# Reciprocal roots of a layer norm on VectorE alone, and one inverse-transform bank moved, in a Fourier-layer tokenizer

## The chip, the cores and the metric

The kernel runs on one core of a Trainium2 chip. The metric is the device time of one execution in microseconds (us); the runs of a kernel are summed up by their median.

## The reference, cut to what matters

The model turns 64 images of 64 x 64 x 3 into 64 x 64 tokens with a small Fourier network (32 channels, 4 layers), then runs an attention block, a gated feed-forward block, a linear recurrence and a mixture of experts over the tokens. The change lies in the tokenizer:

```python
def layer_norm(x, g, b):
    mu = jnp.mean(x, axis=-1, keepdims=True)
    var = jnp.mean((x - mu) ** 2, axis=-1, keepdims=True)
    return (x - mu) * jax.lax.rsqrt(var + EPS) * g + b
...
h = layer_norm(x @ fc0_w + fc0_b, ln0_g, ln0_b)
h = jnp.transpose(h, (0, 3, 1, 2))
for i in range(LAYERS):
    w1 = w1r[i] + 1j * w1i[i]
    w2 = w2r[i] + 1j * w2i[i]
    x1 = spectral_conv(h, w1, w2)
    x2 = jnp.einsum('bchw,oc->bohw', h, conv_w[i]) + conv_b[i][None, :, None, None]
    h = x1 + x2
    h = jnp.transpose(h, (0, 2, 3, 1))
    h = layer_norm(h, ln_g[i], ln_b[i])
    if i < LAYERS - 1:
...
```

`spectral_conv` is a two-dimensional Fourier transform of which 24 x 12 modes are kept, a 32 x 32 complex mixing of channels for each mode, and the inverse transform. Every layer norm needs one reciprocal root for each pixel.

## The kernel before, in words

**Tiling.** The 64 images go in 4 groups of 16, and a group in 2 units of 8 images. A group runs an embedding stage, three layers in a hardware loop, a last layer and the MLP (`program`, line 821); each stage does unit 0 and then unit 1. For each of them there is a *main pass* (`pe_main`, `act_main`, `dve_main`, `pool_main`): one for each unit in the embedding, in each of the three layers and in the last layer, 10 in a group, 40 in all. In the embedding and the three layers a *forward transform* follows (`pe_forward`, `drain_forward`), 32 in all: row transform (line 508), column transform (line 522), mixing (line 539).

**A main pass** handles 16 chunks of 128 partitions x 512 columns. The engines run instruction lists written out by hand and meet at semaphores only:

- TensorE writes chunk c into one of six PSUM banks (`wide[c % 6]`: four of `main`, two of `aux`). In the embedding that is one matmul (line 446), in the layers an inverse column transform (line 453) and a channel matmul (line 456). A bank is written again only when the chunk six before it has been scaled (`main_free`).
- ScalarE squares the bank into `sq` (line 725), VectorE sums the squares over 32 channels (line 703). The means are already zero, since the weights are centred.
- The roots come in two ways. For chunks 0 and 1 of every four, GpSimd adds EPS (line 757) and raises to the power -0.5 (line 760), one chunk at a time. For chunks 2 and 3, VectorE runs nine small instructions for both chunks together behind the reduce and the scaling of the fourth (`dve_newton`, lines 662 to 679).
- VectorE scales chunk c - 3 behind the reduce of chunk c (`scale`, line 694, with `wait_rstd`), into one of two `xn` buffers. After the last reduce the scalings 13, 14 and 15 follow.
- TensorE transposes the scaled chunk (line 464), five chunks later in its own list; ScalarE applies gain, bias and GELU (line 737). In the three layers TensorE also transposes the result back (line 472) and ScalarE copies it into `pix` (line 743); the row transform reads that.

**Inverse row transform.** Towards the end of a main pass TensorE also does eight banks of the *next* unit's inverse row transform (`pe_inverse`, line 423) in the two `aux` banks, even ones drained by VectorE, odd ones by ScalarE (`drain_inverse`, line 598). `inv_banks(c)` says which bank belongs behind which step of the list: banks 0 to 3 behind steps 15 to 18, banks 4 and 5 behind step 19, 6 and 7 behind step 20. In the layers step 21 has only the last transposes back. Bank 0 waits until chunk 11 has been scaled, since `aux` held chunks 10 and 11.

The forward transform begins with a wait for both drains:

```python
            if nxt is not None:
                for j in range(2):
                    pe.wait_ge(inv_free[j], inv_of(g, *nxt) + AX_C)
```

In the embedding it then transposes 64 tiles (line 495) in turn through two `aux` and two `tp` banks; in the layers it starts at the row transform, whose results go to `main[0]` and `main[1]`. The column transform uses `main[2]`, `main[3]`, then `tp`, and for its last third (y = 2) the two `aux` banks.

The spectrum goes out and back by DMA on SP's queue (`sp_spectrum`), for use by the inverse banks of the next main pass. A line of the profile that belongs to a helper (598 is `copy`) holds many tiles.

Of the kernel before, what the change touches and what calls it, by code (L numbers as in the profile page):

```python
# [106 lines left out]
def tokenizer(nc, t, tok, named):  # L107
# [9 lines left out]
    with ctx:  # L117
# [31 lines left out]
        mhalf = sb("mhalf", [128, 16])  # L149
# [56 lines left out]
        with nc.Block() as block:  # L206
# [43 lines left out]
            def _(dve):  # L250
# [6 lines left out]
                dve.memset(mhalf[:, :], -0.5)  # L257
# [76 lines left out]
        main_full, main_free, sq_full, red_done, var_done, rstd_done, newton, tp_full, tp_free = (  # L334
            sem(n) for n in ("main_full", "main_free", "sq_full", "red_done", "var_done", "rstd_done", "newton",
# [43 lines left out]
        def inv_banks(c):  # L379
            return {NCH - 1: (0,), NCH: (1,), NCH + 1: (2,), NCH + 2: (3,), NCH + 3: (4, 5), NCH + 4: (6, 7)}.get(c, ())  # L380
# [49 lines left out]
        def pe_main(pe, g, s, u, l, nxt):  # L430
# [7 lines left out]
            for c in range(NCH + LAG + (1 if turns else 0)):  # L438
# [36 lines left out]
                if nxt is not None:  # L475
                    for k in inv_banks(c):
# [137 lines left out]
        def drain_forward(eng, j, g, s, u, l):  # L614
            _, n = base_of(g, s, u, l)
            fwd = (g * (LAYERS * UNITS) + (0 if s == 0 else l * UNITS + UNITS) + u)
            if s == 0:
                n = n + AX_EMBED
                for k in range(j, 4 * AX_ROWS, 2):
# [3 lines left out]
                    else:  # L623
                        eng.wait_ge(row_full[j], (g * UNITS + u) * AX_ROWS + (START + k // 4 + 1))
                    copy(eng, j, pv[:, :, :, 4 * k:4 * k + 4].rearrange("p c a r -> p a c r"),
                         (aux if first else tp)[j][:, :].rearrange("p (r a c) -> p a c r", r=4, a=NA)).then_inc(
# [27 lines left out]
        def dve_newton(dve, m, c):  # L654
# [8 lines left out]
            dve.wait_ge(main_free, after(m, c, 4))  # L663
            dve.wait_ge(newton, done + 4)
            dve.tensor_scalar(y.bitcast(I32), v.bitcast(I32), -0.5, float(0x5f3759df), ALU.mult, ALU.add).then_inc(newton, 4)
            dve.wait_ge(newton, done + 8)
            dve.tensor_tensor(w, y, y, ALU.mult).then_inc(newton, 4)
            dve.wait_ge(newton, done + 12)
            dve.tensor_tensor(w, w, v, ALU.mult).then_inc(newton, 4)
            dve.wait_ge(newton, done + 16)  # L670
            dve.scalar_tensor_tensor(out=w, in0=w, scalar=-10 / 3, in1=w, op0=ALU.add, op1=ALU.mult).then_inc(newton, 4)
            dve.wait_ge(newton, done + 20)
            dve.scalar_tensor_tensor(out=y, in0=w, scalar=5.0, in1=y, op0=ALU.add, op1=ALU.mult).then_inc(newton, 4)
            dve.wait_ge(newton, done + 24)
            dve.scalar_tensor_tensor(out=w, in0=y, scalar=-0.5 * CUBIC ** 2, in1=y, op0=ALU.mult, op1=ALU.mult).then_inc(newton, 4)
            dve.wait_ge(newton, done + 28)
            dve.tensor_tensor(w, w, v, ALU.mult).then_inc(newton, 4)
            dve.wait_ge(newton, done + 32)
            dve.scalar_tensor_tensor(out=y, in0=w, scalar=1.5, in1=y, op0=ALU.add, op1=ALU.mult).then_inc(newton, 4)

        def wait_rstd(dve, m, c):

            if c % 4 < 2:
                dve.wait_ge(rstd_done, m + 4 * (c // 4) + 2 * (c % 4 + 1))
            else:
                dve.wait_ge(newton, (m - START) * NEWTON_OPS + (START + (c // 4 + 1) * 4 * NEWTON_OPS))

        def dve_main(dve, g, s, u, l, nxt):
# [10 lines left out]
            for c in range(NCH):  # L699
# [7 lines left out]
                if c % 4 == 3:  # L707
# [8 lines left out]
        def act_main(act, g, s, u, l, nxt):  # L716
# [4 lines left out]
            for c in range(NCH + LAG + (1 if turns else 0)):  # L721
                if c < NCH:
# [3 lines left out]
                                   scale=CH ** -0.5 / (CUBIC if c % 4 >= 2 else 1)).then_inc(sq_full, 1)  # L726
# [18 lines left out]
                if nxt is not None:  # L745
                    for k in inv_banks(c - 1):
                        if k % 2:
                            drain_inverse(act, 1, g, *nxt, k)
            if nxt is not None and not turns:
                drain_inverse(act, 1, g, *nxt, 7)  # L750

        def pool_main(pool, g, s, u, l):
            m, _ = base_of(g, s, u, l)
            for c in range(NCH):
                if c % 4 < 2:
                    pool.wait_ge(red_done, m + c + 1)
                    pool.tensor_tensor(var[:, c % 4, :], ssum[:, c % 4, :], eps[:, :], ALU.add).then_inc(var_done, 2)  # L757
                    pool.wait_ge(var_done, m + 4 * (c // 4) + 2 * (c % 4 + 1))
                    pool.wait_ge(main_free, after(m, c, 4))
                    pool.tensor_tensor(rstd[:, c % 4, :], var[:, c % 4, :], mhalf[:, :], ALU.pow).then_inc(rstd_done, 2)  # L760
# [927 lines left out]
```

## Time and profile before

| | us |
|---|---|
| median of 3 runs (lowest, highest) | 4886.96 (4884.19, 4889.06) |
| the profiled execution | 4915.42 |
| its span, first to last instruction | 4913.6 |
| TensorE busy | 4008.5 |
| VectorE busy | 2260.9 |
| ScalarE busy | 2096.9 |
| GpSimd busy | 1057.9 |
| mean granted clock of TensorE, as a share of full speed | 0.909 |

The profiled execution took somewhat longer than the runs that were timed without a profile. In a row of the timeline the first number is the start in us from the begin of the span, the second the duration; then engine, line, operation, output <- input, shape, count, and in brackets the idle time of that engine just before it with what ended it. PE is TensorE, DVE VectorE, ACT ScalarE, POOL GpSimd. An fp32 matmul shows as two instructions. In a row of stretches the columns are the stretch, its length, busy us and number of instructions for PE, PE's weight loads, DVE, ACT and POOL, then the granted clock (1.00 is 2.4 GHz, 0.50 is 1.2 GHz), DMA share and GB/s.

### The profile page before, as it was taken

The numbers are of one execution on the slowest core, as the hardware profiler recorded it, in microseconds if no ns is written. First come the engines' busy times: TensorE is split into PE (matmuls) and PEld (weight loads), VectorE is DVE, ScalarE is ACT, GpSimd is POOL, SyncE is SP. The second block draws the span as 40 slices with busy tenths as digits, with TensorE's granted clock in tenths as the row PEclk, the third lists the DMA queues.
The fourth block names the chain that finished last, engine by engine and source line by source line (L and its number), as shares of the span: only waits on it lengthen the run. The fifth ranks groups of instructions, "written<-read, shape, count | busy, mean of one in ns | idle before, by whom it ended". The sixth has DMA issues, their size and how long they took to land. (4 is left out here: it accounts for less than half of the span.)

```text
span 4913.6 us, 101922 instructions
## 1 busy us (share of the span) xinstructions
PE 4008.5 (82%) x39344; PEld 3080.9 (63%) x39344; DVE 2260.9 (46%) x4667; ACT 2096.9 (43%) x3178; POOL 1057.9 (22%) x700
## 2 busy tenths in 40 slices
PE   0189999996899999968999999689999995857268
PEld 0068788842788888427888884278887832853146
DVE  6554443431544345224443442244434422787666
ACT  1254444465544444654443446544444463221113
POOL 0032322321223223212332232223223320000020
PEclk9999999998999999989999999899999997779679
DMA  9501201200022022000210220002102101000000
GB/s 206 159 22 59 79 21 60 79 1 16 21 72 67 21 69 69 1 16 21 79 60 21 75 64 2 15 21 79 60 21 79 59 2 31 1 1 1 0 1 9
DMA packets 168682, 213.28 MB, mean 43 GB/s; under 512 B 156402, under 2 KB 158679, under 8 KB 159874
## 3 DMA queue, kind: packets, MB, share of 16 engines
q1 hardware_dynamic: 166514, 182.84, 12.8%
q10 hardware_dynamic: 1680, 23.60, 1.9%
q8 instruction: 347, 5.69, 0.5%
q14 instruction: 141, 1.16, 0.1%
HBM read 147.28 MB, written 59.12 MB: 42 GB/s over the span
## 5 line engine op out<-in xcount | busy, mean ns | idle before, releaser
L760 POOL TENSOR_TENSOR rstd<-var,mhalf 128x16 f32<-128x16 f32 x320 | 931.2, 2910 | 44.1 <-POOL var L757 4.4
L757 POOL TENSOR_TENSOR var<-ssum,eps 128x16 f32<-128x16 f32 x320 | 69.4, 217 | 2923.9 <-DVE ssum L703 2923.9
L737 ACT ACTIVATE h<-tp,gb 128x512 f32<-128x512 f32 x640 | 553.7, 868 | 297.6 <-PE tp L464 296.1
L703 DVE TENSOR_REDUCE ssum<-sq 128x16 f32<-128x512 f32 x640 | 436.2, 683 | 484.5 <-ACT sq L725 481.0
L508 PE MATMUL main<-fwd_w,pix 128*128 128x96 f32 x4096 | 513.9, 293 | 42.1 <-ACT zq L598 35.1
L508 PEld LDWEIGHTS main<-fwd_w,pix 128*128 128x128 f32 x4096 | 509.6, 209 | 48.8 <-ACT pix L743 40.1
L456 PEld LDWEIGHTS main<-convw,h 128*128 128x128 f32 x3072 | 407.4, 209 | 161.2 <-issue 161.2
L464 PE MATMUL tp<-ident,xn 128*128 128x128 f32 x2560 | 423.6, 292 | 77.5 <-DVE xn L694 71.9
L725 ACT ACTIVATE sq<-main 128x512 f32<-128x512 f32 x480 | 286.5, 599 | 441.2 <-PE main L456 394.3
L456 PE MATMUL main<-convw,h 128*128 (+1 forms) x3072 | 455.7, 300 | 0.0
L423 PE MATMUL aux<-inv_r,yd 96*48 96x64 f32 x8192 | 417.1, 256 | 9.5 <-DVE zq L598 4.5
L464 PEld LDWEIGHTS tp<-ident,xn 128*128 128x128 f32 x2560 | 314.9, 150 | 163.3 <-DVE xn L694 130.6
L423 PEld LDWEIGHTS aux<-inv_r,yd 96*48 96x48 f32 x8192 | 388.9, 185 | 44.7 <-issue 32.5
L453 PE MATMUL main<-zq,inv_w 48*128 48x512 f32 x768 | 292.3, 679 | 88.1 <-DVE xn L694 47.8
L598 DVE COPY t_w<-main 128x384 f32<-128x384 f32 (+1 forms) x192 | 94.2, 490 | 558.3 <-PE main L508 477.4
L694 DVE TENSOR_TENSOR xn<-main,rstd 128x512 f32<-128x512 f32 x480 | 327.0, 683 | 20.3 <-POOL rstd L760 10.9
L598 ACT COPY t_w<-main 128x384 f32<-128x384 f32 (+1 forms) x192 | 81.6, 425 | 580.1 <-PE main L508 479.7
L743 ACT COPY pix<-tp 128x512 f32<-128x512 f32 x384 | 221.4, 576 | 56.0 <-PE tp L472 56.0
L472 PE MATMUL tp<-ident,h 128*128 128x128 f32 x1536 | 241.9, 282 | 0.0
L598 DVE COPY zq<-aux 112x512 f32<-112x512 f32 x128 | 88.1, 688 | 265.6 <-PE aux L423 265.6
L573 PE MATMUL main<-h,f1w 32*128 32x512 f32 x1024 | 181.5, 671 | 14.1 <-ACT pix L768 9.6
L539 PE MATMUL main<-xs,mixw 128*64 128x32 f32 x6144 | 188.9, 223 | 0.0
(240 smaller groups left out, 5868.6 us busy)
## 6 DMA issues: line engine op xcount, KB each, us to landing
mixw<-mix_scratch SPq DMA_DIRECT2D x16, 4608.0 KB, 17.8
y_scratch<-t_w SPq DMA_DIRECT2D x256, 144.0 KB
yd<-y_scratch SPq DMA_DIRECT2D x32, 1152.0 KB, 7.5
mix_scratch<-mixw SPq DMA_DIRECT2D x64, 288.0 KB, 4.8
mixw<-mix_scratch ACTq DMA_DIRECT2D x1, 4608.0 KB, 13.7
h<-in_L_tok_w1r ACTq DMA_DIRECT2D x6, 576.0 KB, 10.1
h<-in_L_tok_w1i ACTq DMA_DIRECT2D x6, 576.0 KB, 10.4
h<-in_L_tok_w2r ACTq DMA_DIRECT2D x6, 576.0 KB, 18.3
```

The source lines that it names most:

```text
L423: mm = pe.matmul(aux[j][64 * half:64 * half + 48, 64 * i:64 * i + 64], ydv[:, u, 8 * e + i, :, :, a].rearrange("p s n -> p (s n)"), inv_r[ ...
L453: pe.matmul(wide[(c + half) % 6][:, :], inv_w[rows, :], zq[rows, 256 * c:256 * c + 512], start=True, stop=False)
L456: mm = pe.matmul(bank[:, 128 * i:128 * i + 128], h[:, (u * S + 4 * c + i) * 128:(u * S + 4 * c + i) * 128 + 128], convw[:, layer, :] if l ...
L464: mm = pe.transpose(tp[0 if turns else d % 2][:, 128 * i:128 * i + 128], xn[:, d % 2, 128 * i:128 * i + 128], ident[:, :])
L472: mm = pe.transpose(tp[1][:, 128 * i:128 * i + 128], h[:, (u * S + 4 * d + i) * 128:(u * S + 4 * d + i) * 128 + 128], ident[:, :])
L508: mm = pe.matmul(main[j][:, 48 * i:48 * i + 96], pv[:, c0 + i, 2 * ap:2 * ap + 2, :].rearrange("p a r -> p (a r)"), fwd_w[:, :], start=Tru ...
L598: return eng.tensor_copy(out, in_) if j == 0 else eng.copy(out, in_)
L694: dve.tensor_tensor(xn[:, d % 2, :].rearrange("p (n c) -> p n c", c=CH), wide[d % 6][:, :].rearrange("p (n c) -> p n c", c=CH), rstd[:, d ...
L703: dve.tensor_reduce(ssum[:, c % 4, :], sq[:, c % 2, :].rearrange("p (n c) -> p n c", c=CH), AX.X, ALU.add).then_inc(red_done, 1)
L725: act.activation(sq[:, c % 2, :], wide[c % 6][:, :], ACT.Square, scale=CH ** -0.5 / (CUBIC if c % 4 >= 2 else 1)).then_inc(sq_full, 1)
L737: act.activation(out, in_, fn, bias=gb[:, 1, stage:stage + 1] if l is None else gb[:, 1, bass.ds(stage, 1)], scale=gb[:, 0, stage:stage + ...
L760: pool.tensor_tensor(rstd[:, c % 4, :], var[:, c % 4, :], mhalf[:, :], ALU.pow).then_inc(rstd_done, 2)
```

## The change

All roots are computed by the nine Newton instructions on VectorE, behind every odd chunk for that chunk and the one before; the instructions have the same shape, 128 x 32, as before. `pool_main`, the GpSimd program that called it, its two semaphores and the constant `mhalf` go. ScalarE's squares get the same scale for all chunks.

In the layers, bank 7 of the inverse row transform moves from step 20 to step 21, behind the last transposes back. The forward transform no longer waits for the drains of the inverse banks at its begin; it waits for them at the first use of `aux` in its column transform (y = 2). For this the embedding's first transposes use `main[0]` and `main[1]` in place of `aux`.

```diff
         def inv_banks(c):
-            return {..., NCH + 3: (4, 5), NCH + 4: (6, 7)}.get(c, ())
+        def inv_banks(c, turns):
+            return {..., NCH + 3: (4, 5), NCH + 4: (6,) if turns else (6, 7), NCH + 5: (7,)}.get(c, ())
...
         def pe_forward(pe, g, s, u, l, nxt):
             m, n = base_of(g, s, u, l)
-            if nxt is not None:
-                for j in range(2):
-                    pe.wait_ge(inv_free[j], inv_of(g, *nxt) + AX_C)
...
-                        mm = pe.transpose((aux if first else tp)[j][:, 128 * i:128 * i + 128],
+                        mm = pe.transpose((main if first else tp)[j][:, 128 * i:128 * i + 128],
...
+                        if nxt is not None and y == 2 and ap == 0:
+                            pe.wait_ge(inv_free[b], inv_of(g, *nxt) + AX_C)
...
         def dve_newton(dve, m, c):
-            v, y, w = (x[:, 2:4, :].rearrange("p k n -> p (k n)") for x in (var, rstd, newton_w))
-            done = (m - START) * NEWTON_OPS + (START + (c // 4) * 4 * NEWTON_OPS)
+            p = slice(c % 4 - 1, c % 4 + 1)
+            v, y, w = (x[:, p, :].rearrange("p k n -> p (k n)") for x in (var, rstd, newton_w))
+            done = (m - START) * NEWTON_OPS + (START + (c // 2) * 2 * NEWTON_OPS)
             dve.wait_ge(red_done, m + c + 1)
-            dve.tensor_scalar(v, ssum[:, 2:4, :].rearrange("p k n -> p (k n)"), EPS / CUBIC ** 2, None, ALU.add).then_inc(newton, 4)
+            dve.tensor_scalar(v, ssum[:, p, :].rearrange("p k n -> p (k n)"), EPS / CUBIC ** 2, None, ALU.add).then_inc(newton, 2)
...
-            if c % 4 < 2:
-                dve.wait_ge(rstd_done, m + 4 * (c // 4) + 2 * (c % 4 + 1))
-            else:
-                dve.wait_ge(newton, (m - START) * NEWTON_OPS + (START + (c // 4 + 1) * 4 * NEWTON_OPS))
+            dve.wait_ge(newton, (m - START) * NEWTON_OPS + (START + (c // 2 + 1) * 2 * NEWTON_OPS))
...
-                if c % 4 == 3:
+                if c % 2:
                     dve_newton(dve, m, c)
...
-                                   scale=CH ** -0.5 / (CUBIC if c % 4 >= 2 else 1)).then_inc(sq_full, 1)
+                                   scale=CH ** -0.5 / CUBIC).then_inc(sq_full, 1)
...
-        def pool_main(pool, g, s, u, l):
...
-                    pool.tensor_tensor(rstd[:, c % 4, :], var[:, c % 4, :], mhalf[:, :], ALU.pow).then_inc(rstd_done, 2)
...
-            @block.gpsimd
-            def _(pool):
...
```

## Rows read from the trace of the kernel before

**Rows 1.** The page, part 1: busy us, share, instructions.
```profile
PE 4008.5 (82%) x39344; PEld 3080.9 (63%) x39344; DVE 2260.9 (46%) x4667; ACT 2096.9 (43%) x3178; POOL 1057.9 (22%) x700
```

**Rows 2.** VectorE's timeline, embedding pass, second unit: start, us, what, idle before.
```profile
318.31 0.69 DVE L703 TENSOR_REDUCE ssum<-sq 128x16 f32<-128x512 f32 x1 [0.17 <-ACT sq L725]
...
322.18 0.17 DVE L662 TENSOR_SCALAR var<-ssum 128x32 f32<-128x32 f32 x1
...
324.69 0.69 DVE L703 TENSOR_REDUCE ssum<-sq 128x16 f32<-128x512 f32 x1
...
325.29 0.68 DVE L694 TENSOR_TENSOR xn<-main,rstd 128x512 f32<-128x512 f32 x1
...
347.46 0.69 DVE L694 TENSOR_TENSOR xn<-main,rstd 128x512 f32<-128x512 f32 x1
```

**Rows 3.** TensorE's timeline, a layer pass.
```profile
501.71 1.12 PE L453 MATMUL main<-zq,inv_w 48*128 48x512 f32 x2 [1.42 <-DVE xn L694]
...
506.50 1.13 PE L453 MATMUL main<-zq,inv_w 48*128 48x512 f32 x4
...
525.89 1.66 PE L423 MATMUL aux<-inv_r,yd 96*48 96x64 f32 x32
```

**Rows 4.** Timelines of TensorE and ScalarE, end of that layer pass.
```profile
543.61 0.66 PE L472 MATMUL tp<-ident,h 128*128 128x128 f32 x4
...
544.30 0.59 ACT L743 COPY pix<-tp 128x512 f32<-128x512 f32 x1 [2.33 <-PE tp L472]
...
545.72 17.55 PE L508 MATMUL main<-fwd_w,pix 128*128 128x96 f32 x128 [1.45 <-ACT zq L598]
```

**Rows 5.** Line 508: TensorE idle before it (us, times), until.
```profile
  ACT zq L598: 35.1, 24
```

**Rows 6.** TensorE's timeline, embedding, second unit: first transposes and row transform.
```profile
361.55 1.06 PE L495 MATMUL aux<-ident,h 128*128 128x128 f32 x8 [0.73 <-issue]
...
369.60 14.50 PE L508 MATMUL main<-fwd_w,pix 128*128 128x96 f32 x128 [0.87 <-ACT pix L598]
```

**Rows 7.** Stretches around 545: us, busy by engine, granted clock, DMA share, GB/s.
```profile
540.00:543.00 3.00, 3.00 (x60) 2.82 (x59) 0.69 (x1) 1.74 (x3) 0.00 (x0) 1.00 0.02 5
...
546.00:548.00 2.00, 2.00 (x11) 2.00 (x11) 0.00 (x0) 0.00 (x0) 0.00 (x0) 0.50 0.00 0
...
552.00:554.00 2.00, 2.00 (x19) 2.00 (x19) 0.00 (x0) 0.48 (x1) 0.00 (x0) 0.97 0.00 0
```

**Rows 8.** Line 508 alone, sums over stretches: 24 in layers, 8 in embeddings.
```profile
sum 480.00, PE 397.88 PEld 394.65; mean PE 16.58 PEld 16.44
...
sum 160.00, PE 116.02 PEld 114.94; mean PE 14.50 PEld 14.37
```

**Rows 9.** TensorE and VectorE, embedding pass, first unit.
```profile
234.49 7.16 PE L446 MATMUL main<-yd 97*128 97x512 f32 x8 [0.86 <-ACT yd L598]
...
238.93 0.69 DVE L703 TENSOR_REDUCE ssum<-sq 128x16 f32<-128x512 f32 x1 [0.93 <-ACT sq L725]
...
268.90 1.28 DVE L694 TENSOR_TENSOR xn<-main,rstd 128x512 f32<-128x512 f32 x2
...
269.64 1.97 PE L464 MATMUL tp<-ident,xn 128*128 128x128 f32 x8 [2.39 <-DVE xn L694]
```

**Rows 10.** VectorE, last pass, second unit.
```profile
1005.74 0.69 DVE L703 TENSOR_REDUCE ssum<-sq 128x16 f32<-128x512 f32 x1 [0.21 <-ACT sq L725]
...
1040.44 1.28 DVE L694 TENSOR_TENSOR xn<-main,rstd 128x512 f32<-128x512 f32 x2
```

**Rows 11.** VectorE, the layer pass of rows 3.
```profile
493.38 0.69 DVE L703 TENSOR_REDUCE ssum<-sq 128x16 f32<-128x512 f32 x1 [0.21 <-ACT sq L725]
...
500.98 0.68 DVE L694 TENSOR_TENSOR xn<-main,rstd 128x512 f32<-128x512 f32 x1
```

**Rows 12.** TensorE, a layer pass with a longer low clock.
```profile
1845.68 2.02 PE L453 MATMUL main<-zq,inv_w 48*128 48x512 f32 x2 [1.42 <-DVE xn L694]
...
1892.95 16.13 PE L508 MATMUL main<-fwd_w,pix 128*128 128x96 f32 x128 [1.45 <-ACT zq L598]
```

More of the change, by code:

```diff
@@ L331, in _ @@
                 mm.then_inc(p_pe, 1)
-        main_full, main_free, sq_full, red_done, var_done, rstd_done, newton, tp_full, tp_free = (
-            sem(n) for n in ("main_full", "main_free", "sq_full", "red_done", "var_done", "rstd_done", "newton",
+        main_full, main_free, sq_full, red_done, newton, tp_full, tp_free = (
+            sem(n) for n in ("main_full", "main_free", "sq_full", "red_done", "newton",
                                   "tp_full", "tp_free"))
@@ L475, in pe_main @@
                 if nxt is not None:
-                    for k in inv_banks(c):
+                    for k in inv_banks(c, turns):
                         pe_inverse(pe, g, *nxt, m, k)
@@ L625, in drain_forward @@
                     copy(eng, j, pv[:, :, :, 4 * k:4 * k + 4].rearrange("p c a r -> p a c r"),
-                         (aux if first else tp)[j][:, :].rearrange("p (r a c) -> p a c r", r=4, a=NA)).then_inc(
+                         (main if first else tp)[j][:, :].rearrange("p (r a c) -> p a c r", r=4, a=NA)).then_inc(
                              aux_free[j] if first else row_free[j], 1)
@@ L666, in dve_newton @@
+            dve.tensor_tensor(w, w, v, ALU.mult).then_inc(newton, 2)
             dve.wait_ge(newton, done + 8)
-            dve.tensor_tensor(w, y, y, ALU.mult).then_inc(newton, 4)
+            dve.scalar_tensor_tensor(out=w, in0=w, scalar=-10 / 3, in1=w, op0=ALU.add, op1=ALU.mult).then_inc(newton, 2)
+            dve.wait_ge(newton, done + 10)
+            dve.scalar_tensor_tensor(out=y, in0=w, scalar=5.0, in1=y, op0=ALU.add, op1=ALU.mult).then_inc(newton, 2)
             dve.wait_ge(newton, done + 12)
-            dve.tensor_tensor(w, w, v, ALU.mult).then_inc(newton, 4)
+            dve.scalar_tensor_tensor(out=w, in0=y, scalar=-0.5 * CUBIC ** 2, in1=y, op0=ALU.mult, op1=ALU.mult).then_inc(newton, 2)
@@ L670, in dve_newton @@
+            dve.wait_ge(newton, done + 14)
+            dve.tensor_tensor(w, w, v, ALU.mult).then_inc(newton, 2)
             dve.wait_ge(newton, done + 16)
[L671 to L679, printed above, removed]
+            dve.scalar_tensor_tensor(out=y, in0=w, scalar=1.5, in1=y, op0=ALU.add, op1=ALU.mult).then_inc(newton, 2)
         def wait_rstd(dve, m, c):
-            if c % 4 < 2:
-                dve.wait_ge(rstd_done, m + 4 * (c // 4) + 2 * (c % 4 + 1))
-            else:
-                dve.wait_ge(newton, (m - START) * NEWTON_OPS + (START + (c // 4 + 1) * 4 * NEWTON_OPS))
+            dve.wait_ge(newton, (m - START) * NEWTON_OPS + (START + (c // 2 + 1) * 2 * NEWTON_OPS))
@@ L745, in act_main @@
                 if nxt is not None:
-                    for k in inv_banks(c - 1):
+                    for k in inv_banks(c - 1, turns):
                         if k % 2:
                             drain_inverse(act, 1, g, *nxt, k)
-            if nxt is not None and not turns:
+            if nxt is not None:
                 drain_inverse(act, 1, g, *nxt, 7)
-        def pool_main(pool, g, s, u, l):
[L753 to L759, printed above, removed]
-                    pool.tensor_tensor(rstd[:, c % 4, :], var[:, c % 4, :], mhalf[:, :], ALU.pow).then_inc(rstd_done, 2)
         def act_mlp(act, g, u):
@@ L879, in _ @@
                 dve.memset(xs[:, :], 0.0).then_inc(xs_zero, 1)
[L880 removed]
+                for i, counter in enumerate((*aux_full, *aux_free, *inv_full, *inv_free, *row_full, *row_free, turn_full, turn_free, main_full, main_free, sq_full, red_done, newton,
                                              tp_full, tp_free, fc1_full, g1_done, fc2_full, g2_done)):
@@ L892, in _ @@
                 drains(act, 1, act_main, act_mlp)
-            @block.gpsimd
-            def _(pool):
-                def one(s):
-                    def f(g, l=None):
-                        for u in range(UNITS):
-                            pool_main(pool, g, s, u, l)
-                    return f
-                program(pool, one(0), one(1), one(LAYERS), lambda g: None)
             @block.sync
```

11 lines of the change are left out of this document (5 added, 6 removed).

## The prediction

> **What bounds the kernel now.** The page first: TensorE is busy 82% of the span, VectorE 46%, GpSimd 22% [rows 1]. These shares are averages; what the change is worth is read from the timelines of the tokenizer's three kinds of main pass (embedding, layer, last), and no work after the tokenizer is touched. A pass handles 16 chunks: square on ScalarE, reduce on VectorE, a root, a scaling on VectorE three chunks later, a transpose on TensorE.
>
> In VectorE's timeline of an embedding pass [rows 2] the scaling starts 0.60 us after the reduce (324.69 to 325.29), the next instruction 0.60 us after a scaling, and one block of nine Newton steps lasts from 322.18 to the next reduce at 324.69: 2.51 us for two chunks. Four chunks today cost VectorE 8 x 0.60 + 2.51 = 7.31 us. With a block for every pair it is **4 x 0.60 + 2.51 = 4.91 us a pair**, 9.82 us for four chunks, whatever the other engines do.
>
> In a layer pass two cycles of four chunks take TensorE from 506.50 to 525.89, 19.39 us, or 4.85 a pair [rows 3]. So there TensorE is the bound and VectorE would come level with it. In an embedding pass TensorE has less to do, and VectorE bounds already.
>
> At the end of each layer pass TensorE does two inverse banks and the last transposes back, and then stands still until ScalarE has drained the last bank: the row transform (L508) starts 1.45 us after TensorE went idle [rows 4]. This happens 24 times, 35.1 us in all [rows 5]; an embedding transform waits only 0.87 us [rows 6]. The granted clock matters more: 1.00 up to 543, 0.50 (1.2 GHz) behind the gap, 0.97 again from 552 [rows 7]. The same 128 matmuls take 14.50 us on average over the 8 embedding transforms, which keep full speed behind their shorter gap, and 16.58 over the 24 in the layers [rows 8].
>
> **Part 1, the moved bank.** Bank 7 (32 matmuls; such a bank takes 1.66 us [rows 3]) goes behind the last transposes back, and the row transform no longer waits for the two drains. Today those transposes start at 543.61 and ScalarE's copy of them ends at 544.89 [rows 4], 1.28 us later; bank 7 now fills that time, so nothing is left to wait for. Saved: the 35.1 us of gaps (bounds 24 and 36: half a microsecond each may remain). The drain of bank 7 is now waited for late in the column transforms; queued behind that wait is their last third, covered by the row transform's 14.5 us in between against a drain of 0.59 us [rows 4]. No DMA is moved and no queue passed.
>
> The clock falls at the gap and not in the banks and transposes ahead of it. I take it that it no longer falls: 397.88 - 24 x 14.50 = 49.9 us. Bounds 0 and 49.9; I take the upper end, because the embedding transforms, the second of them also behind inverse banks, keep their 14.50.
> By the Trainium skill (TensorE: Matmul & The Clock Gate, section "HAM oscillation — how this bites in real kernels") the idle gaps that hurt are much longer than this one; by that rule the gap is not what drops the clock, and the 49.9 us would stay lost. The trace speaks against it with a mean of 16.58 us behind the longer gap and 14.50 behind the shorter [rows 8].
>
> In the second embedding unit the transform's first transposes also wait for the drain, 0.73 us after the last bank [rows 6]; some 0.65 go: 4 x 0.65 = 2.6 us. Their banks in main in place of aux cost nothing: all 16 scalings have released main by then.
>
> **Part 2, the roots.** GpSimd's powers go, but what is late next is VectorE itself. I walk its chain.
>
> Embedding, second unit [rows 2]: reduce 1 at 318.31, block (0,1) from 318.91 to 321.42; reduces 2 and 3 and scaling 0, 1.80 us, block (2,3) to 325.73; six more pairs of 4.91 end at 355.19. Today the scaling behind the last block starts at 347.46: **+7.7 us**. First unit [rows 9]: reduce 1 at 238.93, block (0,1) ends at 242.04, (2,3) at 246.35, the last at 275.81 against 268.90: +6.9. All later work hangs on these last scalings. Four groups: 4 x 14.6 = 58.4 us (bounds 50 and 62).
>
> Last pass [rows 10]: reduce 1 at 1005.74, block (0,1) ends at 1008.85, (2,3) at 1013.16, the last at 1042.62 against 1040.44: +2.2, in eight passes 17.6 us (bounds 12 and 20).
>
> Layer pass [rows 11]: reduce 1 at 493.38, block (0,1) ends at 496.5, and scaling 1 starts at 501.4 instead of 500.98, so the stall of 1.42 us at TensorE's seventh chunk [rows 3] grows by 0.42. After that 4.91 against 4.85 keeps VectorE just behind: block (12,13) ends at 525.35, scaling 11 at 526.65, and inverse bank 0, which starts at 525.89 now, is 0.8 late. This stage keeps its clock; in the others TensorE loses 1.6 us or more to a low clock after the stall, VectorE catches up, and only 0.42 to 0.6 is left. 24 x 0.55 = 13.2 us (bounds 10 and 20).
>
> The longer stall can prolong that low clock. From the seventh chunk to the row transform a stage takes 44.01 us without a fall [rows 3, 4] and 47.27 with a long one [rows 12], 3.26 us for two steps of 1.63. By the same difference twelve stages have at most one step today and could gain one; I take four, 6.5 us (bounds 0 and 20; no row shows the new stalls).
>
> The memset that is dropped costs nothing: it lies in the set-up, far ahead of the first group.
>
> **Sum.** -35.1 - 49.9 - 2.6 + 58.4 + 17.6 + 13.2 + 6.5 = +8.1 us. The profiled execution took 4915.4 us, 28 more than the median of the runs, 4887.0; it would become 4923.5, the median 4895. A measurement of this kernel can tell about 0.2%, 9.8 us, from no change; the forecast is just inside that.
>
> **Rivals.**
> *VectorE's lateness in the layers is covered.* TensorE at half clock after the stall is late by itself, and if the low stretch ends at a time of its own, a longer stall only moves idle time into it. Then 13.2 and 6.5 fall away: 4875, faster. For it: the long fall of [rows 12] is common. Against: the scaling that releases the seventh chunk is later in each stage. Chance 0.30.
> *TensorE becomes the bound of the embedding.* Half clock has followed a wait of 2.39 us there; at it eight matmuls, four chunks' worth, took 7.16 us and the eight transposes of two chunks 1.97 us [rows 9]: 1.79 + 0.98 = 2.77 us a chunk, 5.5 a pair, over 4.91. Today such waits come once in four chunks, the new ones with every pair. If the clock stays there, 8 passes x 7 pairs x 0.6 us = 35 us, 4930; for three fifths of the time 21 us, 4916: slower. It decides once most of a pass runs at half clock; against it, TensorE is three chunks ahead of VectorE and catches up at full clock. Chance 0.18.
> *The clock falls before the row transform all the same*, because it is the short matmuls and transposes, not the gap, that bring it down: 4895 + 50 = 4945, slower. No row shows this stretch without its gap. Chance 0.10.
> That GpSimd stays in use is excluded: no instruction of it is left in the passes.
>
> **How the numbers follow.** The forecast has 0.40 and, by its bounds, 4881 to 4909; three tenths of it lie over 9.8 us. Faster by over 0.2%: most of the first rival and 0.02 for gains not seen, 0.28. Slower: 0.12 of the forecast with 0.18 and 0.10, 0.40. Within: 0.32. The range, 4868 to 4930, takes in the first two rivals and leaves out the third.
>
> **What would show it.** Right: L508 at 14.50 us in every stage, with no wait on ScalarE's drain; Newton blocks of 2.51 us, twice as many; embedding passes about 7 us longer, last passes 2, the seventh chunk's stall near 1.85 us. Wrong: L508 still near 16.6 us; blocks well under 2.5 us now that GpSimd is still; embedding matmuls mostly at half clock.

## The result and the profile after

The changed kernel takes **4969.42 us** (median of 4 runs, 4967.85 to 4971.57) against 4888.01 us for the kernel before in the same session (4884.19 to 4898.63): ratio **1.0145, interval 1.0124 to 1.0166**. The two medians alone make 1.0167; by them it is slower by 81 us, where the forecast had +8. The kernel before was run again in each of the later sessions, with medians of 4893 to 4903 us; against those the change costs 66 to 76 us, so differences between two sessions are good to some 10 us. The profiled execution took 4971.57 us, its span is 4969.8 us, the mean granted clock 0.901.

The page of the kernel after, part 1 and three groups of part 5 (the last column: idle time ahead of the group and what ended most of it):

```profile
PE 4042.2 (81%) x39344; PEld 3074.3 (62%) x39344; DVE 2509.1 (50%) x6104; ACT 2108.2 (42%) x3178; POOL 62.5 (1%) x60
...
L503 PE MATMUL main<-fwd_w,pix 128*128 128x96 f32 x4096 | 464.8, 276 | 7.0 <-ACT pix L595 7.0
...
L451 PE MATMUL main<-zq,inv_w 48*128 48x512 f32 x768 | 313.8, 698 | 104.7 <-DVE xn L689 62.9
L689 DVE TENSOR_TENSOR xn<-main,rstd 128x512 f32<-128x512 f32 x480 | 326.9, 682 | 17.2 <-PE tp L462 14.0
```

GpSimd is nearly gone and VectorE has 248 us more than in [rows 1]. The row transform, now line 503, waits for the embedding's last copy only, 7.0 us in all; the 35.1 us of [rows 5] are gone, and 464.8 us for 32 transforms is 14.5 each, where the 24 in the layers took 16.58 [rows 8]. What is lost shows in TensorE's waits. First the view of waits of the kernel before, then of the kernel after (total us, times, longest):

```profile
PE tp L464 <- DVE xn L694: 71.9, 52, 2.4
PE main L453 <- DVE xn L694: 47.8, 36, 2.0
```

```profile
PE tp L462 <- DVE xn L689: 111.8, 77, 2.9
PE main L451 <- DVE xn L689: 62.9, 32, 2.0
PE aux L421 <- DVE xn L689: 12.3, 20, 1.9
```

TensorE waits for VectorE's scalings everywhere: for transposes (mostly embedding), at the inverse column transform (layer and last passes), and now also at the inverse banks, 12.3 us where the wait for scalings was 3.0 us before.

A table of stretches, worked out from TensorE's timelines (each from the first matmul of a pass to the first of what follows, so that a row transform ends where its column transform begins; a layer pass holds the wait ahead of its row transform, an embedding pass the transposes ahead of its matmuls and those ahead of its row transform). "Median time" is that of the runs, "profiled" the one execution from which the stretches are read. The kernel before was profiled twice. The rows below the second are those of the experiments, which are described further on.

| us | median time | profiled | 8 embedding passes | 32 row transforms | 24 layer passes | 8 last passes |
|---|---|---|---|---|---|---|
| before | 4888.0 | 4915.4 | 437.5 | 508.6 | 1430.7 | 383.2 |
| after | 4969.4 | 4971.6 | 500.8 | 459.6 | 1439.2 | 417.8 |
| before, second profile | one run | 4894.3 | 438.8 | 497.9 | 1423.7 | 380.0 |
| bank and wait only | 4828.7 | 4823.5 | 435.9 | 459.5 | 1385.4 | 389.8 |
| wait only | 4853.7 | 4860.3 | 434.8 | 459.6 | 1411.6 | 399.5 |
| roots only | 5043.7 | 5054.0 | 518.8 | 506.9 | 1464.0 | 414.1 |
| bank, wait, embedding's roots | 4890.6 | 4888.7 | 504.8 | 459.5 | 1380.6 | 389.1 |
| after, all blocks late | 4976.6 | 4979.4 | 515.0 | 459.6 | 1427.2 | 427.4 |
| after, one block late | 4948.5 | 4946.8 | 504.6 | 459.5 | 1412.6 | 416.4 |
| after, short blocks | 4763.5 | 4762.0 | 460.7 | 459.6 | 1336.8 | 354.3 |
| before, block late | 4858.7 | 4856.5 | 466.8 | 494.2 | 1365.9 | 377.5 |
| bank, wait, all blocks late | 4797.7 | 4779.7 | 452.7 | 459.5 | 1336.4 | 377.9 |
| bank, wait, one block late | 4778.0 | 4784.0 | 433.0 | 459.5 | 1355.7 | 379.6 |
| the same, short blocks | 4712.1 | 4713.2 | 408.1 | 459.6 | 1333.4 | 358.3 |

What is left of each span (column transforms, mixing, MLP and all later work) is 2148 to 2154 us in every row.

### The profile page after: what moved, and what is told of

Its sections match the earlier page's. It is cut to its first block and busy times, and to the rows that moved or that the text cites. A ratio compares the mean times of both kernels' runs of the same rounds, so it can differ in the third digit from the quotient of the medians.

```text
span 4969.8 us, 104406 instructions
## 1 busy us (share of the span) xinstructions
PE 4042.2 (81%) x39344; PEld 3074.3 (62%) x39344; DVE 2509.1 (50%) x6104; ACT 2108.2 (42%) x3178; POOL 62.5 (1%) x60
## 5 line engine op out<-in xcount | busy, mean ns | idle before, releaser
L462 PE MATMUL tp<-ident,xn 128*128 128x128 f32 x2560 | 448.0, 304 | 115.0 <-DVE xn L689 111.8
L454 PEld LDWEIGHTS main<-convw,h 128*128 128x128 f32 x3072 | 423.3, 216 | 170.9 <-issue 170.9
L454 PE MATMUL main<-convw,h 128*128 (+1 forms) x3072 | 472.8, 307 | 0.0
L503 PE MATMUL main<-fwd_w,pix 128*128 128x96 f32 x4096 | 464.8, 276 | 7.0 <-ACT pix L595 7.0
L462 PEld LDWEIGHTS tp<-ident,xn 128*128 128x128 f32 x2560 | 329.8, 156 | 221.0 <-DVE xn L689 189.2
L503 PEld LDWEIGHTS main<-fwd_w,pix 128*128 128x128 f32 x4096 | 459.8, 192 | 10.3 <-DVE pix L595 8.6
L421 PE MATMUL aux<-inv_r,yd 96*48 96x64 f32 x8192 | 422.2, 258 | 16.9 <-DVE xn L689 12.3
L451 PE MATMUL main<-zq,inv_w 48*128 48x512 f32 x768 | 313.8, 698 | 104.7 <-DVE xn L689 62.9
L595 ACT COPY t_w<-main 128x384 f32<-128x384 f32 (+1 forms) x192 | 81.8, 426 | 505.1 <-PE main L503 405.1
L451 PEld LDWEIGHTS main<-zq,inv_w 48*128 48x128 f32 x768 | 87.5, 198 | 175.2 <-DVE xn L689 105.3
L470 PEld LDWEIGHTS tp<-ident,h 128*128 128x128 f32 x1536 | 187.3, 146 | 1.6
```

The costliest lines, as they stand in the source:

```text
L421: mm = pe.matmul(aux[j][64 * half:64 * half + 48, 64 * i:64 * i + 64], ydv[:, u, 8 * e + i, :, :, a].rearrange("p s n -> p (s n)"), inv_r[ ...
L451: pe.matmul(wide[(c + half) % 6][:, :], inv_w[rows, :], zq[rows, 256 * c:256 * c + 512], start=True, stop=False)
L454: mm = pe.matmul(bank[:, 128 * i:128 * i + 128], h[:, (u * S + 4 * c + i) * 128:(u * S + 4 * c + i) * 128 + 128], convw[:, layer, :] if l ...
L462: mm = pe.transpose(tp[0 if turns else d % 2][:, 128 * i:128 * i + 128], xn[:, d % 2, 128 * i:128 * i + 128], ident[:, :])
L470: mm = pe.transpose(tp[1][:, 128 * i:128 * i + 128], h[:, (u * S + 4 * d + i) * 128:(u * S + 4 * d + i) * 128 + 128], ident[:, :])
L503: mm = pe.matmul(main[j][:, 48 * i:48 * i + 96], pv[:, c0 + i, 2 * ap:2 * ap + 2, :].rearrange("p a r -> p (a r)"), fwd_w[:, :], start=Tru ...
```

## The experiments

### The change taken apart

**The bank and the wait alone**, with the old roots: the diff's parts in `inv_banks`, `pe_forward` and `drain_forward`.

> The moved bank and the moved wait alone, with the old roots. Theory A (the bank saves what the trace of after shows, 35 us of gaps, 50 us of row transforms at low clock and 2 to 3 us in the embedding, whatever the roots do): about 4888 - 87 = 4801 us, all 32 row transforms at 14.5 us. Rival B (the clock at the row transform stays up only because the slower roots change what goes before): row transforms stay near 16.6 us, only the gaps go, about 4851 us.

Measured: 4828.67 us against 4897.04, ratio 0.9857 (0.983 to 0.9884). All row transforms run at full clock and in the layers no gap is left ahead of them, so theory A's mechanism holds; its size does not. The last passes grew from 380.0 to 389.8 us against the second profile of the kernel before, and its row transforms had lost only 38.4 us there (497.9 - 459.5).

**The roots alone**, with bank 7 and the wait as before: the other parts of the diff.

> All roots by Newton steps on VectorE, banks and waits as before. Theory A (the two parts add up): 4888 + 81 + 87, about 5056 us, with the seventh-chunk stall at 2.00 us in every layer and last pass and the row transforms still at 16 to 18 us. Rival C (the roots cost what the forecast said, 95 us, and something else in after lost the rest): about 4983 us.

Measured: 5043.74 us, ratio 1.0289 (1.0259 to 1.0319). The two parts add up: -68.4 and +146.7 make +78.3; the whole change is +81.4 against the kernel before of its own session and +72.4 against that of this one (4897.04). So nothing beyond the noise lies between them (each part's interval is about 14 us to either side), and the roots, priced at 95.7 us, are what was undersized. The row transforms were expected at 16 to 18 us throughout, but 8 of the 24 in the layers kept 14.50 behind the unchanged wait, as this one:

```profile
858.65 14.50 PE L506 MATMUL main<-fwd_w,pix 128*128 128x96 f32 x128 [1.45 <-ACT zq L596]
```

**The wait alone.** Bank 7 stays at step 20; the forward transform waits late:

```diff
-            if nxt is not None:
-                for j in range(2):
-                    pe.wait_ge(inv_free[j], inv_of(g, *nxt) + AX_C)
...
+                        if nxt is not None and y == 2 and ap == 0:
+                            pe.wait_ge(inv_free[b], inv_of(g, *nxt) + AX_C)
```

> Old roots, bank 7 stays ahead of the last transposes back, only the wait for the drains moves to the last third of the column transform. TensorE then waits only for ScalarE's copy of the last transposes, some 0.8 us instead of 1.45. If the length of the gap decides on the clock (Theory A): row transforms near 14.5 us, gaps of 0.8 us left, about 4888 - 50 - 16 - 3 = 4819 us. If the short matmuls and transposes ahead of it bring the clock down (Rival D): row transforms stay at 16.6 us, about 4869 us.

Measured: 4853.67 us, ratio 0.9898 (0.9867 to 0.9929). TensorE's timeline of this run, end of a layer pass:

```profile
540.57 0.66 PE L472 MATMUL tp<-ident,h 128*128 128x128 f32 x4
541.90 4.37 PE L505 MATMUL main<-fwd_w,pix 128*128 128x96 f32 x37 [0.68 <-ACT pix L742]
```

The last row ends with the view, at 37 of the 128 instructions. A gap of 0.68 us, for ScalarE's copy, stays ahead of the row transform, and all 32 transforms are at full clock (459.6 us). Rival D falls: at this place it was the longer wait, not the matmuls ahead of the transform, that brought the clock down where it fell. Yet theory A's time was missed by 35 us. Some 12 of them are the 50 us taken for the row transforms, which the second profile has at 38.3; 19.5 are in the last passes, where the clock falls instead. In a last pass of this run, TensorE's timeline and then stretches of 3 us (the number ahead of the DMA share is the granted clock):

```profile
944.79 1.81 PE L453 MATMUL main<-zq,inv_w 48*128 48x512 f32 x2 [1.19 <-DVE xn L693]
```

```profile
942.00:945.00 3.00, 1.81 (x8) 0.81 (x7) 2.50 (x8) 1.27 (x2) 1.88 (x3) 1.00 0.93 242
945.00:948.00 3.00, 3.00 (x9) 1.55 (x9) 0.92 (x2) 0.00 (x0) 2.87 (x3) 0.51 1.07 307
948.00:951.00 3.00, 3.00 (x16) 3.00 (x16) 1.34 (x2) 1.38 (x2) 2.77 (x1) 0.50 0.91 393
```

The same place of the kernel before, whose stall is 1.19 us too, TensorE's timeline and then the stretches:

```profile
962.39 1.12 PE L453 MATMUL main<-zq,inv_w 48*128 48x512 f32 x2 [1.19 <-DVE xn L694]
```

```profile
960.00:963.00 3.00, 1.81 (x6) 0.59 (x4) 2.69 (x8) 1.02 (x2) 1.88 (x3) 1.00 0.95 242
963.00:966.00 3.00, 3.00 (x25) 2.56 (x24) 1.26 (x3) 1.31 (x3) 2.87 (x3) 1.00 0.97 287
```

Behind a wait of the same length the clock goes to 0.50 (1.2 GHz) in one kernel and stays at 1.00 (2.4 GHz) in the other. A fall that is taken away at one wait can turn up at another: 19.5 us in the last passes here, 9.8 us in the run before.

**The kernel before, once more**, for a second profile.

> The kernel before once more, unchanged, for a second profiled execution. Theory A (the profiled execution of before was 28 us over its median because its clock fell more often after the stalls of the main passes): passes without a stall over 1.3 us keep their lengths, those with one differ by steps of 1.6 us. Rival E (the profiler itself adds the 28 us): again about 4915 us, with the same lengths everywhere.

Measured: 4894.29 us, row transforms 497.9 us in place of 508.6, layer passes 1423.7 in place of 1430.7. The first profile, on which the forecast rests, had its 21 us more in just the stretches where the clock falls. Rival E, by which the profiler adds them, falls.

**The embedding's roots.** Bank and wait moved, the new roots in the embedding alone (GpSimd works there on a tile that nobody reads). The main lines of the edit, against the kernel before; `dve_newton2` is the block of the changed kernel:

```diff
+                if s == 0 and c % 2:
+                    dve_newton2(dve, m, c)
-                if c % 4 == 3:
+                elif c % 4 == 3:
                     dve_newton(dve, m, c)
```

> The bank's and the wait's move (4828.67 us), with the new roots in the embedding alone; there GpSimd works on a tile that nobody reads, and layer and last passes have the old roots. Theory A: the embedding passes with their first transposes go from 54.5 to 62.6 us, 8 x 8.1 = +65: 4893, and the rest of what separates the whole change from the moved bank (4969 - 4829 - 65 = 76 us) is that of layer and last passes. Rival I, the embedding's loss is mostly one that follows from the state in which the passes before leave TensorE's clock: under +35, below 4865.

Measured: 4890.59 us, so the embedding's roots cost **61.9 us** over the moved bank alone (theory A: 65), and rival I falls. Layer and last passes have the other 78.8, a difference of medians from two sessions; the table's profiles give 81.8 for them (1439.2 - 1385.4 and 417.8 - 389.8).

### Why the layer passes lose so much

A layer pass of the kernel after, TensorE:

```profile
512.79 2.07 PE L451 MATMUL main<-zq,inv_w 48*128 48x512 f32 x2 [2.00 <-DVE xn L689]
514.79 2.07 PE L454 MATMUL main<-convw,h 128*128 x8
...
540.88 1.66 PE L421 MATMUL aux<-inv_r,yd 96*48 96x64 f32 x32 [0.18 <-DVE xn L689]
...
557.65 1.66 PE L421 MATMUL aux<-inv_r,yd 96*48 96x64 f32 x32
559.24 4.04 PE L503 MATMUL main<-fwd_w,pix 128*128 128x96 f32 x34
```

The same pass, VectorE:

```profile
503.89 0.69 DVE L698 TENSOR_REDUCE ssum<-sq 128x16 f32<-128x512 f32 x1 [0.21 <-ACT sq L720]
504.68 0.18 DVE L660 TENSOR_SCALAR var<-ssum 128x32 f32<-128x32 f32 x1
...
512.05 0.68 DVE L689 TENSOR_TENSOR xn<-main,rstd 128x512 f32<-128x512 f32 x1
...
513.84 0.17 DVE L660 TENSOR_SCALAR var<-ssum 128x32 f32<-128x32 f32 x1
...
514.93 0.19 DVE L667 TENSOR_TENSOR newton_w<-newton_w,var 128x32 f32<-128x32 f32 x1 [0.34 <-DVE newton_w L665]
...
517.53 0.69 DVE L698 TENSOR_REDUCE ssum<-sq 128x16 f32<-128x512 f32 x1 [0.92 <-ACT sq L720]
...
520.63 0.69 DVE L698 TENSOR_REDUCE ssum<-sq 128x16 f32<-128x512 f32 x1 [1.82 <-ACT sq L720]
...
521.84 0.17 DVE L660 TENSOR_SCALAR var<-ssum 128x32 f32<-128x32 f32 x1
...
526.74 0.17 DVE L660 TENSOR_SCALAR var<-ssum 128x32 f32<-128x32 f32 x1
...
536.90 0.17 DVE L660 TENSOR_SCALAR var<-ssum 128x32 f32<-128x32 f32 x1
```

Read the two together (the last row of TensorE's ends with the view). The stall at the seventh chunk (chunk 7 counted from 0, which waits for scaling 1) is 2.00 us, 1.42 in [rows 3]. Behind it TensorE's two matmuls take 2.07 us, 1.12 at full clock. The granted clock of the 7.01 us behind the stall, in the changed kernel and, second, in the kernel before behind the stall of [rows 3]:

```profile
512.79:519.80 7.01, 7.01 (x26) 5.51 (x27) 4.03 (x13) 1.95 (x3) 0.00 (x0) 0.52 0.32 77
```

```profile
501.71:508.72 7.01, 7.01 (x48) 5.33 (x49) 4.37 (x11) 3.54 (x6) 5.85 (x3) 1.00 0.39 93
```

TensorE's slow matmuls hand ScalarE its squares late, and VectorE, which was the late engine, now idles 0.92 + 1.82 = 2.74 us for them. When the squares come, VectorE has a pair of 4.90 us (521.84 to 526.74) against TensorE's own 4.85, so it can't win that back. The block of chunks 12 and 13 begins 33.0 us behind reduce 1. In the other second-unit layer passes VectorE idles 1.1 to 2.8 us in this way.

The longer the stall, the more time TensorE then spends at low clock. The table has the twelve second-unit layer passes of each run: the stall in each pass at this chunk (in the run with 1.77 us two chunks on), and the time at 1.2 GHz by the granted clock, summed over the twelve. The run with all blocks late is left out; its longest wait, 1.95 us, comes later in the pass, and it has 41 us.

| stall, us | runs | us at 1.2 GHz |
|---|---|---|
| 0.3 | before, block late; bank and wait with all blocks late, with one block late, and with that and short blocks | 0 |
| 0.54 | after, short blocks | 10 |
| 1.2 | bank, wait, embedding's roots | 38 |
| 1.42 | before, twice; bank and wait; wait only | 41 to 52 |
| 1.77 | after, one block late | 55 |
| 2.00 | roots only; after | 64 and 68 |

And the 24 layer and 8 last passes, the changed kernel against the run with bank and wait alone, taken apart from TensorE's timelines: of the 81.8 us, 32 are longer waits (over 0.1 us each), 38 are lost to more time at low clock (half of the time that TensorE works at 1.2 GHz), and 12 are a slower pace.

**All blocks late in the changed kernel.** If the stall were the cause, taking scaling 1 out from behind a block should win:

```diff
-                if c % 2:
-                    dve_newton(dve, m, c)
+                if c % 2 == 0 and c:
+                    dve_newton(dve, m, c - 1)
+            dve_newton(dve, m, NCH - 1)
```

> The whole change (4969.42 us), with every Newton block one slot later, behind the reduce and the scaling of the slot that follows; VectorE's instructions are the same in number. Theory E: the stalls of 2.00 us and the half-clock steps behind them, in layer and last passes, are what the change lost beyond VectorE's throughput: 32 stalls shrink by 1.0 to 1.7 us and 2 low-clock steps of 1.63 us a pass go, while the embedding passes keep their 62 us above the old: 4969 - 60 to 110, about 4860 to 4910. Rival H, the added VectorE time itself makes the length of all passes: the stall only moves to another chunk, 4950 to 4970.

Measured: 4976.56 us, ratio 1.0159 (1.0131 to 1.0187): nothing won, close to rival H's 4950 to 4970. The layer passes gained 12 us, embedding and last passes lost 24. The stall at the seventh chunk is gone, and this stands in TensorE's timeline instead, at the third inverse bank:

```profile
550.31 1.79 PE L421 MATMUL aux<-inv_r,yd 96*48 96x64 f32 x32 [1.95 <-DVE zq L595]
```

The blocks of chunks 12, 13 and 14, 15 now stand in neighbouring slots ahead of VectorE's first drain.

**One block late in the changed kernel**, that of chunks 2 and 3, in layer and last passes:

```diff
-                if c % 2:
+                if c % 2 and not (s and c == 3):
                     dve_newton(dve, m, c)
+                if s and c == 4:
+                    dve_newton(dve, m, 3)
```

> The whole change (4969.42 us); only the block of chunks 2 and 3 runs one slot later, behind the reduce and the scaling of slot 4, in layer and last passes alone; all other blocks stand where the change has them, so that no two blocks come close together at the end of a pass. Theory E2: all blocks late (4976.56) lost at the end of the passes what it won at the seventh chunk, since the blocks of chunks 12, 13 and 14, 15 then stood in neighbouring slots ahead of the first inverse drains (a wait of 1.95 to 2.42 us there). With the one block moved the stall of 2.00 us at the seventh chunk goes to about 1.1 and no new one comes: 28 to 32 passes win 0.9 us and 1 to 2 steps of 1.63 us, 4969 - 50 to 100, about 4870 to 4920. Rival H, VectorE's added time makes the length of the passes wherever the block stands: 4955 to 4975.

Measured: 4948.51 us, ratio 1.0105 (1.0076 to 1.0135). It wins 21 us, less than theory E2's 50 to 100 and more than rival H allows: both missed. The stall moved two chunks on:

```profile
517.77 1.27 PE L451 MATMUL main<-zq,inv_w 48*128 48x512 f32 x2 [1.76 <-DVE xn L689]
```

It is shorter, and the 24 layer passes have 135 us at 1.2 GHz in place of 192 and are 27 us shorter. What TensorE loses to the low clock in them is then no more than in the run with bank and wait alone (67 us in both); yet they are 27 us longer than there (1412.6 against 1385.4), most of it, 23 us, slower pace. Where a block stands decides which chunk is late, hardly how late.

**Short blocks in the changed kernel**: the last three of the nine small steps left out (the second Newton step, so the roots are coarser).

```diff
-NEWTON_OPS = 9
+NEWTON_OPS = 6
...
-            dve.scalar_tensor_tensor(out=w, in0=y, scalar=-0.5 * CUBIC ** 2, in1=y, op0=ALU.mult, op1=ALU.mult).then_inc(newton, 2)
...
-            dve.tensor_tensor(w, w, v, ALU.mult).then_inc(newton, 2)
...
-            dve.scalar_tensor_tensor(out=y, in0=w, scalar=1.5, in1=y, op0=ALU.add, op1=ALU.mult).then_inc(newton, 2)
```

> The whole change with the last three of the nine small steps of each Newton block left out (the second Newton step, so the roots are coarser): a block of 2.51 us becomes about 1.6 us. Theory A, VectorE sets the pace of the embedding passes: a pair of 4.91 us becomes 4.0 us, 8 passes x 4 pairs x 0.9 = -28 us there, and the stalls of layer and last passes shrink by 0.9 us with their low-clock steps, -30 to -70: about 4870 to 4910. Rival B, TensorE at half clock sets the embedding's pace: the embedding passes keep their 62.6 us each, 4900 to 4940.

Measured: **4763.53 us**, ratio 0.9728 (0.9701 to 0.9755): 206 us less than with nine steps, far more than theory A's 60 to 100 and against rival B. VectorE and TensorE of this run in a layer pass:

```profile
502.49 0.17 DVE L660 TENSOR_SCALAR var<-ssum 128x32 f32<-128x32 f32 x1
...
504.32 0.69 DVE L692 TENSOR_REDUCE ssum<-sq 128x16 f32<-128x512 f32 x1 [0.18 <-ACT sq L714]
```

```profile
501.44 1.12 PE L451 MATMUL main<-zq,inv_w 48*128 48x512 f32 x2 [0.54 <-DVE xn L683]
```

The reduce behind the block now waits 0.18 us for ScalarE: VectorE has slack again. The stall is 0.54 us and the clock stays up (1.12). The layer passes fall by 102 us, the last passes by 64, the embedding by 40. Rival B falls, and with the two runs before it, in which the same number of instructions stood elsewhere and won little or nothing, this shows that VectorE's instruction time makes the loss in all three kinds of pass. Not all of the 206 us are that loss, though: the roots cost 147 us in all, and layer and last passes are now shorter than with bank and wait alone (1336.8 and 354.3 against 1385.4 and 389.8). A short block also takes away most of the stall that the kernel before already had there.

### Versions that beat both kernels

**The kernel before with its block late** (chunks 2 and 3 of every four, one slot later):

> The kernel before (4888 us), with the Newton block of chunks 2 and 3 one slot later. Theory E: the stalls of 1.19 to 1.42 us at the seventh chunk go under 0.5 us (32 x 1.0 = -30) and the clock stays up behind them in the layer passes where it had fallen (some -20 to -40); the gap ahead of the row transforms stays, and its 50 us of half clock: 4820 to 4840. Rival G, scaling 1 is held by GpSimd's power: 4888.

Measured: 4858.67 us, ratio 0.9922 (0.9896 to 0.9949). The layer passes won 58 us, so rival G falls; the embedding passes lost 28, which theory E had left out, so its time was missed.

**Bank and wait moved, all of VectorE's blocks late, old roots:**

> The bank's and the wait's move alone (4828.67 us), with the Newton block of chunks 2 and 3 one slot later, behind the reduce and the scaling of the slot that follows: scaling 1 is no longer behind nine small steps. Theory E, the stall at the seventh chunk (1.2 to 2.0 us) is VectorE's block ahead of scaling 1, and the fall of the clock behind it comes from that stall: the stall goes under 0.5 us in all 24 layer passes and 8 last passes, and the clock stays up behind it: 32 x 1.0 us of stall, and 1 to 2 low-clock steps of 1.63 us in most passes, some 60 to 80 us in all: 4750 to 4770. Rival F, the stall goes but the clock falls behind another wait of the same pass all the same: only the stalls' 30 us come, about 4800. Rival G, scaling 1 is held by GpSimd's power: the stall stays, about 4828.

Measured: 4797.72 us, ratio 0.9799 (0.9773 to 0.9826). Layer and last passes won 61 us as theory E says, the embedding gave 17 back, by a profile that lies 18 us under the median; the time is rival F's, though its reason isn't seen.

**The same with one block late, in layer and last passes only:**

> The bank's and the wait's move with the old roots (4828.67 us), and only the block of chunks 2 and 3 one slot later, in layer and last passes alone. In the run with all of VectorE's blocks late the layer passes took 1336 us in place of 1385 and the embedding passes 453 in place of 436. Theory E: with the embedding left as it was 17 us more are won than there (4797.72): 4770 to 4790. Rival: later blocks, not the first, made the layer passes shorter: 4800 to 4830.

Measured: **4777.99 us**, ratio 0.9747 (0.9718 to 0.9775), as theory E says. The embedding is back at 433.0 us, but the layer passes took 1355.7 us against 1336.4 with all blocks late. Whether the later blocks had a share in those isn't shown: that profile lies 18 us under its median and this one 6 above.

**And with short blocks** (the coarser roots again)**:**

> The moved bank and wait with the old division of the roots and the first block one slot later (4777.99 us), with the last three of the nine small steps of each block left out, as in the short blocks of the whole change (4763.53). Theory A, VectorE's chain sets the length of the embedding passes with half the blocks too: 8 passes x 4 blocks x 0.9 us = -28; in the layer passes, where nearly no stall is left, TensorE is the bound and only the stalls of 1.43 us in the first units shrink, -10 to -25: 4725 to 4745. Rival, GpSimd's powers of the other two chunks set the pace by now: under -10, 4768 or more.

Measured: **4712.08 us**, ratio 0.9611 (0.959 to 0.9632), the fastest of all. The embedding won 25 us and the layer passes 22, as theory A says; the last passes won another 21, which it had not counted, so the time lies under its range. GpSimd's powers do not set the pace yet.

## Why the prediction was wrong

It forecast +8.1 us; against the median of the session of the parts (4897.04) the whole change costs 72.4. The 64.3 us between that and the forecast, part by part:

**The moved bank and wait: -68.4 in place of -87.6.** The mechanism was right: no gap, no wait on ScalarE's drain, 14.5 us in every transform. Two things were off. "Saved: 397.88 - 24 x 14.50 = 49.9 us" came from a profile 28 us over the median, and "it would become 4923.5, the median 4895" took all of that surplus off again. But part of the surplus lay in these very transforms: the second profile has 38.4 us to save there, 11.5 less. The step failed by counting a surplus as constant that the change removes. Another 9.8 us is the clock that falls in the last passes instead, which no step allowed for. The run with the wait alone keeps full clock behind 0.68 us, where 1.45 us had brought it down. So the rule of the Trainium skill weighed there (TensorE: Matmul & The Clock Gate, section "HAM oscillation — how this bites in real kernels"), by which the 49.9 us would have stayed lost, is not borne out.

**Embedding: +61.9 in place of +58.4**, at the upper end of its bounds (64.9 by the table's profiles). From reduce 1 to the scaling behind the last block the second unit takes 37.29 us (322.91 to 360.20 in the rows below) in place of 29.15 in [rows 2], +8.1 where +7.7 was forecast.

```profile
322.91 0.69 DVE L698 TENSOR_REDUCE ssum<-sq 128x16 f32<-128x512 f32 x1 [0.17 <-ACT sq L720]
323.70 0.18 DVE L660 TENSOR_SCALAR var<-ssum 128x32 f32<-128x32 f32 x1
...
360.20 0.69 DVE L689 TENSOR_TENSOR xn<-main,rstd 128x512 f32<-128x512 f32 x1
```

The rival of TensorE at half clock did not decide: VectorE waits for no other engine between these rows, and short blocks took 5.0 us off each of these passes.

**Layer and last passes: +78.8 in place of 37.3** (13.2, 6.5 and 17.6). Here the reasoning failed, first of all in the price of the low clock: "twelve stages have at most one step today and could gain one; I take four, 6.5 us", and nothing for it in the last passes. By the working above, the longer waits came to 32 us, close to the 30.8 forecast, but the low clock to 38. The 24 layer passes have 44 steps of 1.63 us behind the stalled chunk; with bank and wait alone they have 27, and those in the kernel before's first profile 34. That is 17 or 10 more in place of four.

It failed, second, in the sentence "TensorE loses 1.6 us or more to a low clock after the stall, VectorE catches up, and only 0.42 to 0.6 is left". At the first inverse bank TensorE does wait only 0.18 us, but because it is late itself; VectorE doesn't win time while TensorE is slow, it idles for squares that come late, 2.74 us in the pass shown. Two engines at 4.90 and 4.85 us a pair have no slack, so what one loses the other can't take back: that is the slower pace, 12 us here, and 23 us in the layer passes of the run with one block late. "Block (12,13) ends at 525.35" puts its begin at 522.84, 29.46 us behind reduce 1 [rows 11]; it came 33.01 us behind it (503.89 to 536.90). Of the 3.55 us between them 2.74 are idle time; most of the rest are blocks with one slow step, as at 514.93, and a first block that starts 0.79 us behind its reduce (503.89 to 504.68) in place of 0.60. That start, not seen in the rows before, since there a scaling stood between, is also why the stall is 2.00 us and not 1.85. In the last passes the same holds: "the last at 1042.62 against 1040.44" let TensorE keep its clock. In the first unit's it had full clock behind the stall in the kernel before (963 to 966 above), and there it falls now, behind a stall of 2.00 us:

```profile
963.00:966.00 3.00, 2.00 (x11) 1.01 (x9) 2.17 (x11) 1.53 (x3) 0.00 (x0) 1.00 0.94 229
966.00:969.00 3.00, 1.99 (x2) 0.50 (x2) 2.69 (x8) 0.00 (x0) 0.00 (x0) 0.61 1.30 336
969.00:972.00 3.00, 3.00 (x15) 2.99 (x15) 1.32 (x7) 0.60 (x1) 0.00 (x0) 0.50 0.92 393
```

The rivals fared no better. The first (lateness covered) had the coupling the wrong way round, and the third (the clock falls before the row transform) did not happen. Most of what the prediction named as signs of being right is in the trace: no wait and 14.50 us at the row transforms, blocks of 2.51 us, embedding passes 8 us longer. The last passes grew by 3.5 us each where 2 were named, and the stall is 2.00 us where 1.85 was; the time is still far outside the range. The signs told of each step, none of the low clock behind the stalls or of the coupling between two engines.

## What to carry to other kernels

When an engine that waits now and then is loaded until its period equals that of the engine it feeds, a stall costs more than its own length: here the longer waits cost 32 us, and the low clock of TensorE behind them another 38, during which the loaded engine idled and had no slack to take the time back. Moving the work about mostly moves the stall; fewer instructions remove it (three of nine small ones were worth 206 us here).

By the Trainium skill (VectorE: DVE Perf Modes, section "The DRAIN you can't avoid") a VectorE instruction does not start until the pipeline behind the one before is empty, and leaving out the semaphores between chained instructions does not change that. The trace agrees for the chained small steps, of which 0.19 us each took 0.29 to 0.30 us from start to start; no run here leaves their semaphores out. For a reduce and the scaling behind it, which doesn't read its result, the trace doesn't agree: the scaling starts after 0.60 us, before the reduce's 0.69 are over [rows 2]. Two chained steps of the pass shown above:

```profile
505.26 0.19 DVE L665 TENSOR_TENSOR newton_w<-rstd 128x32 f32<-128x32 f32 x1
505.56 0.19 DVE L667 TENSOR_TENSOR newton_w<-newton_w,var 128x32 f32<-128x32 f32 x1
```

Last, profile a kernel twice before a saving is taken from a single execution that lies above the median.

## What the runs showed that was not expected

- A single wait's length does not decide whether the clock falls, though over many passes longer waits bring more of it. Ahead of the row transforms in the layers, 0.68 us and the embedding's 0.87 us never dropped it. A wait of 1.45 to 1.54 us did so in 24 of 24 in the first profile of the kernel before and in 23 of 24 in the second, but in 18 of 24 with its block late and in 16 of 24 with the roots alone. And 1.19 us at the seventh chunk kept 1.00 in the last passes of the kernel before and gave 0.50 in those of the run with the wait alone. Why the fall moves was not settled.
- The first small step starts 0.79 us behind a reduce whose result it reads (503.89 to 504.68), against 0.60 us behind a scaling.
- Some blocks have one step that comes 0.24 to 0.37 us late with nothing else to wait for than the step before; they occur in the kernel before too. What makes them was not tried.
